# An MoE graph layer on one core: totals per expert ahead of the last ranks, and another order of the step loads

## The reference

```python
logits = tokens @ router_w.T
rw, re = jax.lax.top_k(softmax(logits), 2)
rw = rw / rw.sum(-1)
combine = zeros((N, E)).at[arange(N)[:, None], re].set(rw)
out = tokens
for e in range(8):
    h = gelu(tokens @ w1[e] + b1[e])
    y = h @ w2[e] + b2[e]
    out = out + combine[:, e:e + 1] * y
```

## Time and profile before

| | |
|---|---|
| median of 3 runs | 976.51 us (970.49 to 977.74) |
| the profiled execution, its own time | 976.27 us |
| its span, first to last instruction | 974.5 us |
| mean granted clock of TensorE | 0.933 of 2.4 GHz |
| TensorE (matmul) busy | 857.0 us, 88% |
| VectorE busy | 626.2 us, 64% |
| GpSimd busy | 723.4 us, 74% |
| ScalarE busy | 423.6 us, 43% |

### The profile page before, as it was taken

How to read it: one execution, slowest core, us unless ns; L and a number is a source line. 1 busy time by engine, 2 the same in 40 slices (tenths; PEclk the granted TensorE clock), 3 DMA queues, 4 the chain that set the end, 5 groups by cost and what they waited for, 6 DMA issues and landing times.

```text
span 974.5 us, 19961 instructions
## 1 busy us (share of the span) xinstructions
PE 857.0 (88%) x6332; PEld 528.3 (54%) x6332; DVE 626.2 (64%) x2219; ACT 423.6 (43%) x1156; POOL 723.4 (74%) x506
## 2 busy tenths in 40 slices
PE   3778887988999999999999999999939996499994
PEld 2433433444544454554554555555528996489993
DVE  3699998899466546446446465565666887555552
ACT  3544644333354433434433334344314554167763
POOL 4787888888887887887787888878851156567785
PEclk7699998897899999999999999999969998599997
DMA  9766475445564465454555547563395464568884
GB/s 301 163 111 110 53 144 85 63 60 88 95 126 78 66 116 93 73 84 73 94 84 90 96 57 135 76 124 35 40 301 171 136 192 145 165 111 133 134 136 58
DMA packets 150946, 109.50 MB, mean 112 GB/s; under 512 B 107415, under 2 KB 139354, under 8 KB 150716
## 3 DMA queue, kind: packets, MB, share of 16 engines
q0 software_dynamic: 62496, 26.49, 30.0%
q1 hardware_dynamic: 82272, 71.54, 25.9%
q10 hardware_dynamic: 6076, 10.20, 3.0%
HBM read 65.60 MB, written 42.73 MB: 111 GB/s over the span
## 4 chain that ended last, share of the span: by engine, by line
PE 33%; POOL 13%; issue 5%; DVE 4%; DMA 4%; SPq 1%; ACT 0%; POOLq 0%; DVEq 0%; ACTq 0%
POOL edge_sums L740 13%; PE ps L1585 5%; PE ps L1596 5%; PE ps L1374 4%; PE ps L1514 3%; DMA edge_sums<-sums,addr 3%; PE ps L1181 2%; PE ps L1361 2%; PE ps L1310 2%; PE ps L1324 2%; PE ps L1504 2%; PE ps L1570 1%; PE ps L1350 1%; DMA sums<-edge_sums 1%; PE ps L1249 1%
## 5 line engine op out<-in xcount | busy, mean ns | idle before, releaser
L740 POOL DMA_INDIRECT edge_sums<-sums,addr x360 | 566.2, 1573 | 136.9 <-issue 107.1
L1737 DVE TENSOR_SCALAR oh<-node,dsrc 128x500 bf16<-128x500 int16 (+1 forms) x392 | 116.4, 358 | 73.5 <-PE ps L1374 73.2
L981 ACT ACTIVATE r<-ps 128x500 f32<-128x500 f32 (+1 forms) x224 | 103.4, 549 | 72.0 <-PE ps L1310 71.9
L1374 PE MATMUL ps<-oh,r2t 128*64 128x500 bf16 (+1 forms) x1176 | 130.7, 359 | 1.4 <-DVE oh L1737 1.4
L1181 PE MATMUL ps<-edges,same 128*128 128x65 f32 x720 | 101.4, 287 | 12.5 <-ACT sums L814 4.6
L785 POOL DMA_INDIRECT out_x<-r x56 | 87.8, 1568 | 33.1 <-DVE r L2123 21.4
L1181 PEld LDWEIGHTS ps<-edges,same 128*128 128x128 f32 x720 | 92.1, 200 | 35.8 <-issue 28.1
L1700 DVE TENSOR_TENSOR r2t<-ps,r 125x4096 f32<-125x4096 f32 x25 | 110.3, 4412 | 0.0
L1640 DVE SCALAR_TENSOR_TENSOR same<-srow,src_f,below 128x128 f32<-128x128 int32 x360 | 103.6, 344 | 2.6 <-DMA srow<-in_src_row 1.4
L1374 PEld LDWEIGHTS ps<-oh,r2t 128*64 128x64 bf16 x1176 | 59.1, 110 | 71.2 <-issue 39.2
L1228 PE MATMUL ps<-r2t,r 125*32 125x512 f32 x400 | 60.3, 729 | 34.2 <-DVE r2t L1700 34.2
(11 more groups left out here) (296 smaller groups left out, 1356.3 us busy)
## 6 DMA issues: line engine op xcount, KB each, us to landing
srow<-in_src_row SPq DMA_DIRECT2D x45, 512.0 KB
edges<-in_edge_attr SPq DMA_DIRECT2D x22, 512.0 KB
r<-routed_rows SPq DMA_DIRECT2D x56, 129.0 KB
r<-hpre_rows SPq DMA_DIRECT2D x12, 500.0 KB, 4.5
edge_sums<-sums,addr POOLq DMA_INDIRECT x360, 3.3
r2t<-in_ew SPq DMA_DIRECT2D x4, 1024.0 KB, 8.9
hpre_rows<-r ACTq DMA_DIRECT2D x16, 250.0 KB, 2.3
edge_sums<-r SPq DMA_DIRECT2D x4, 884.0 KB, 13.8
```

Of the source, the lines that this page charges most:

```text
L740: pool.indirect_dma_start(out=tables[k], out_offset=bass.IndirectOffsetOnAxis(ap=addr[:, j:j + 1], axis=0), in_=sums[:, j % OR, :], in_off ...
L981: act.activation(phT[:, R % 2, h, 0:n], bank(BP[h], 128, 0, n), ACT.Square).then_inc(pair_squares, 1)
L1374: m = mm(ps[EA * a:EA * (a + 1), BD * BANK:BD * BANK + n], lhsT=parts3[:, (DCH - 1 - 2 * w // DW) * DW + (2 * w + a) % DW, s, :], rhs=oh[: ...
L1737: v.tensor_scalar(oh[:, (2 * i + a) % OHS, 0:nt * P].rearrange("p (t n) -> p t n", t=nt), node16[:, 0:nt, :], dsrc[:, 2 * w + a:2 * w + a ...
```

## The change

Seven edits go together.

- `carries` gets one more slot, the total behind the last batch. VectorE fills it with one add right behind the last `follow`, and the totals matmul on TensorE reads the three cuts and this slot instead of `carry` and the three cuts. It now stands ahead of the last `ranks`.
- The last `place` moves behind the whole table group, and no longer updates `carry`. TensorE waits for it (`meta_ready`) before the expert steps.
- SyncE no longer writes four pads ahead of the steps. It writes those of experts 0 and 2 behind the load of step 3; ScalarE writes the other six.
- SyncE reads a need at the steps 0, 4 and 6 only, and there takes the need of a later step (3, 5 and 6), which is not smaller. Step 7 waits for all rows (`rows_in` 4), where step 8 did.
- `turns` moves from step 1 to just behind `biases`, ahead of the steps.
- SyncE waits for the last table before it loads the hidden rows of the first four tiles, instead of between these and the weights.
- The two kept cuts move by one slot.

```diff
--- before.py
+++ after.py
@@ -53,6 +53,7 @@
     BASE = 16
     IDLE = E - 1
     EARLY = 8
+    NEEDS = {0: 3, 4: 5, 6: 6}
     SPARE = (0, 22, 44, 66, 88, 110, 128)
     CUTS = (1, 2, 3)
     LEAD = 8
@@ -251,7 +252,7 @@
         picked = carve([P, 2, most, E])
         rows_f = carve([P, 2, most])
         keeps = {n_: carve([P, E * n_]) for n_ in sorted({t1 - t0 for t0, t1 in BATCHES})}
-        carries = carve([P, 1 + len(CUTS), E])
+        carries = carve([P, 2 + len(CUTS), E])
         carry = carries[:, 0, :]
         runner = carve([P, T])
         red = carve([P, T])
@@ -610,10 +611,10 @@
             sp.wait_ge(x1_ready, NP * NB)
             for h in range(2):
                 sp.wait_ge(hpre_stored[h], 16 * MC * NB // 2)
+            sp.wait_ge(tables_back[G4 - 1], 32)
             load_hpre(0)
             load_hpre(1)
 
-            sp.wait_ge(tables_back[G4 - 1], 32)
             for k in range(KC):
                 for dst, w in ((ew1_s, ew1), (ew2_s, ew2)):
                     sp.dma_start(dst[:, k, :].rearrange("p (e n) -> p e n", e=E),
@@ -639,23 +640,28 @@
                     keep_rows(g)
 
 
-            sp.wait_ge(table_ready, 1)
-            for e in range(0, E, 2):
+            def put_pad(e):
+
                 row = sp.value_load(pad_row[0:1, e:e + 1], min_val=128 * IDLE, max_val=128 * IDLE + E * REG - 128)
                 sp.dma_start(routed[bass.ds(row, 128), :], pad_rows[:, :]).then_inc(pads_put, 16)
             sp.wait_ge(table_ready, 2)
 
             def load_steps(sts):
                 for s, h, nth in filter(some, sts):
-                    need = sp.value_load(need_i[0:1, s:s + 1], min_val=1, max_val=1 + 3) if s < EARLY else None
+                    if s in NEEDS:
+                        last = NEEDS[s]
+                        need = sp.value_load(need_i[0:1, last:last + 1], min_val=1, max_val=1 + 3)
                     row = sp.value_load(row_i[0:1, bass.ds(s, 1)], min_val=0, max_val=128 * IDLE + E * REG - 128)
-                    if s < EARLY:
+                    if s in NEEDS:
                         sp.wait_ge(rows_in, need)
-                    elif s == EARLY:
+                    if s == EARLY - 1:
                         sp.wait_ge(rows_in, 1 + 3)
                     wait(sp, xs_ps, s - (SB - 1))
                     wait(sp, idx_ready, s - (SB - 1))
                     sp.dma_start(xs[:, h, :], routed[bass.ds(row, 128), :]).then_inc(xs_loaded[h], 16)
+                    if s == 3:
+                        put_pad(0)
+                        put_pad(2)
                     allow(s - LEAD)
 
             def allow(s):
@@ -1111,7 +1117,7 @@
             act.preload_act_table(ACT.Gelu)
 
             act.wait_ge(table_ready, 1)
-            for e in range(1, E, 2):
+            for e in (1, 3, 4, 5, 6, 7):
                 row = act.value_load(pad_row[0:1, e:e + 1], min_val=128 * IDLE, max_val=128 * IDLE + E * REG - 128)
                 act.dma_start(routed[bass.ds(row, 128), :], pad_rows[:, :]).then_inc(pads_put, 16)
 
@@ -1552,12 +1558,13 @@
             tiles(gnn, 4, [(t1 + 6, lambda b=b: ranks(b)) for b, (t0, t1) in enumerate(BATCHES[:-1])])
             pe.wait_ge(hsum_ready, T)
             pe.wait_ge(x2_ready, T)
+            pe.wait_ge(carried, len(BATCHES))
+            mm(bank(7, 128, 0, (1 + len(CUTS)) * E), lhsT=ones[0:P, :], rhs=carries[:, 1:, :].rearrange("p a e -> p (a e)"), start=True, stop=True).then_inc(ranks_ps, 1)
             ranks(len(BATCHES) - 1)
-            pe.wait_ge(carried, len(BATCHES))
-            mm(bank(7, 128, 0, (1 + len(CUTS)) * E), lhsT=ones[0:P, :], rhs=carries.rearrange("p a e -> p (a e)"), start=True, stop=True).then_inc(ranks_ps, 1)
 
 
             pe.wait_ge(table_ready, 3)
+            pe.wait_ge(meta_ready, len(BATCHES))
             pe.wait_ge(ew_loaded, 16 * (2 * KC + 1))
 
             def xs_T(st):
@@ -2013,11 +2020,14 @@
                 t0, t1 = BATCHES[b]
                 n_ = t1 - t0
                 pk = picked[:, :, 0:n_, :]
-                v.wait_ge(ranks_ps, b + 1)
+                final = b == len(BATCHES) - 1
+                v.wait_ge(ranks_ps, b + 1 + final)
                 link(v.tensor_tensor(pk, bank(0, P, 0, n_ * E).rearrange("p (t e) -> p t e", e=E).unsqueeze(1)
                                      .to_broadcast([P, 2, n_, E]), chosen[:, :, t0:t1, :], ALU.mult))
                 link(v.tensor_reduce(rows_f[:, :, 0:n_], pk, AX.X, ALU.add))
                 v.tensor_copy(row_idx[0:P, :, t0:t1], rows_f[:, :, 0:n_]).then_inc(meta_ready, 1)
+                if final:
+                    return
                 v.wait_ge(meta_ready, b + 1)
                 v.tensor_tensor(carry, carry, upto[:, 0:E * n_].rearrange("p (e t) -> p e t", e=E)[:, :, n_ - 1], ALU.add).then_inc(carried, 1)
                 v.wait_ge(carried, b + 1)
@@ -2045,18 +2055,22 @@
             last_b = len(BATCHES) - 1
             lead(last_b)
             follow(last_b)
+            v.wait_ge(mask_ready, len(BATCHES))
+            n_last = BATCHES[-1][1] - BATCHES[-1][0]
+            v.tensor_tensor(carries[:, 1 + len(CUTS), :], carry, upto[:, 0:E * n_last].rearrange("p (e t) -> p e t", e=E)[:, :, n_last - 1],
+                            ALU.add).then_inc(carried, 1)
             weights(last_b)
-            place(last_b)
-
-            v.wait_ge(ranks_ps, len(BATCHES) + 1)
-            v.tensor_copy(pad_row[:, :], bank(7, 1, 0, E)).then_inc(table_ready, 1)
-            link(v.tensor_tensor(e_n, bank(7, 128, 0, E), reg_start[:, :], ALU.subtract))
+
+            v.wait_ge(ranks_ps, len(BATCHES))
+            total = bank(7, 128, len(CUTS) * E, (1 + len(CUTS)) * E)
+            v.tensor_copy(pad_row[:, :], total[0:1, :]).then_inc(table_ready, 1)
+            link(v.tensor_tensor(e_n, total, reg_start[:, :], ALU.subtract))
             link(v.tensor_scalar(e_i, e_n, 127.0, None, ALU.add))
             link(v.tensor_scalar(e_i, e_i, -128, None, ALU.bitwise_and))
             link(v.tensor_copy(e_pad, e_i))
             link(v.tensor_tensor_scan(e_end, ones[:, 0:E], e_pad, 0.0, ALU.mult, ALU.add))
             v.memset(first_row[:, 0:1], 0.0)
-            v.tensor_scalar(first_row[:, 1:3], bank(7, 1, 2 * E, 4 * E).rearrange("a (k e) -> a k e", k=2)[:, :, 0],
+            v.tensor_scalar(first_row[:, 1:3], bank(7, 1, E, 3 * E).rearrange("a (k e) -> a k e", k=2)[:, :, 0],
                             float(128 * IDLE + 127), None, ALU.subtract)
             v.tensor_scalar(e_n, e_pad, -1.0, float(REG), ALU.mult, ALU.add)
             link(v.tensor_scalar(step_row[:, :], step_row[:, :], e_end[:, E - 1:E], float(128 * NS), ALU.add, ALU.subtract))
@@ -2073,7 +2087,9 @@
             link(v.tensor_reduce(exp_f, past, AX.X, ALU.add))
             v.tensor_scalar(exp_i[:, :], exp_f[0:1, :], float(C), None, ALU.mult).then_inc(table_ready, 1)
             for at_, more in ((0, 256.0), (1, 128.0)):
-                v.scalar_tensor_tensor(cut_n[:, at_, :], bank(7, 1, (1 + at_) * E, (2 + at_) * E), more, reg_start[0:1, :], ALU.add, ALU.subtract)
+                v.scalar_tensor_tensor(cut_n[:, at_, :], bank(7, 1, at_ * E, (1 + at_) * E), more, reg_start[0:1, :], ALU.add, ALU.subtract)
+
+            place(last_b)
 
             def biases():
 
@@ -2137,13 +2153,12 @@
                     w1_copy(step_at(st, 2), cols[-1])
                     output_rows(st)
                     add_b2(step_at(st, -1), cols[-4])
-                    if st[0] == 1:
-                        turns()
             v.wait_ge(table_ready, 3)
             v.wait_ge(ew_loaded, 16 * (2 * KC + 1))
             for s in range(2):
                 w1_copy((s, s, 0), expert_of((s, s, 0)))
             biases()
+            turns()
             steps(v, expert_steps, SB, 2)
```

## The result

The changed kernel took 966.15 us (median of 6 runs, 960.39 to 967.86) where the kernel before took 975.74 in the same comparison (6 runs, 970.49 to 980.13): ratio 0.9894, 95% interval 0.9864 to 0.9924. That is 9.6 us, more than twice the forecast 3.9, and just under the low end of the range (967.5). The profiled execution's own time is 966.35, its span 964.6.

A forecast was written before the change was run, and what follows sets the result against it. TensorE limits most of the span, with a hole between routing and expert steps filled by SyncE's queue. Terms of -3.8 and 0 on 976.27 gave 972.5, with the median's 0.24 972.7; forecast 972.6, range 967.5 to 977.1.

The forecast's parts named there:

- Part 1: Totals ahead of the last ranks: all tables behind the last count scan come 2.26 us earlier.
- Part 2: SyncE's new order: step 0's load issued 3.07 us earlier, at 834.55; first transposes at 837.3 instead of 840.39.
- The cover for place: Last batch's row indices come later, but GpSimd reaches that batch only at 838.46, leaving 4 us of cover.
- needs, pads and step 4: Coarser needs and the moved pads cost nothing, as long as step 4's load keeps 2 us of slack.
- Part 3: Waits table ahead of the steps: copy 2 at 844.8, hidden layer 2 2.5 us earlier (bounds 1.0 and 2.9).
- the 2.31 ahead of layer 4: TensorE's 2.31 us wait at 855.40 for VectorE, made by the waits table in step 1; forecast to go.
- Part 4: Hidden-row reload behind the last table's landing: forecast 0, with -1.5 and +1.5 us as bounds.
- The clock's term: Rise to the higher level at about 850.2: layer 4 gains 4.8 if it moves along, 3.6 if not; taken -3.8.
- rival (1): Clock rises before the wait for copy 2; layer 2 and output 0 run faster, another 1.2: -6.0 us; chance 0.22.

The follow-up runs named there:

- a_reuse_2: Changed kernel in which VectorE keeps the expert registers of the first two weight copies instead of rereading them: 968.41 us, ratio 0.9945 to the kernel before.
- b_warm: Kernel before plus 24 matmuls of 128x128 that nobody reads, behind the totals matmul in TensorE's idle stretch: 974.33 us, ratio 1.0011.

## Why the prediction was wrong

**The steps, one by one.** Part 1 forecast 2.26 us for the tables: 3.27 - 0.99 = 2.28. Part 2 forecast 3.07 for step 0: issued at 830.92, 7.2 behind the scan, instead of 10.4, 3.2 earlier; the transposes 2.96. The cover for place held (5 us; 4 forecast), and needs, pads and step 4 cost nothing. Part 3 forecast copy 2 at 844.8, 17.6 behind the old scan, and 1.6 us of waiting: 17.0 and 1.07, with three loads at 0.59 instead of 0.7. Hidden layer 2 came 2.9 earlier (2.5 forecast, bound 2.9), and the 2.31 ahead of layer 4 went. Part 4 forecast 0, and no effect is shown. The Trainium skill, "DMA: Bandwidth & Descriptors", section "Queues, rings and completion order", says that each DMA engine consumes a queue's descriptors in ring order; by it the order of reload and table makes no odds to the table. The means to the table's add, 16.0 against 15.2 us with a standard error of 0.5, neither bear that out nor contradict it.

**The step that failed: the clock, taken as one value.** The sum took one rise from one profile (850.2) and asked only whether it moves with the work: 3.6 or 4.8, hence 3.8. The clock's term in it is a loss: layer 4 moves by 2.5 + 2.31 = 4.8 without it and by 3.8 with it, so +1.0. In the compared pair the clock rose 16.3 behind the scan instead of 23.0, and hidden layer 4 moved 6.45 = 2.94 + 2.31 + 1.2: the term was a gain of 1.2, as rival (1) had it. But that pair set a late rise against a lucky one. The rise of the old step order alone lay between 18.0 and 23.0, that of the new between 14.3 and 21.5, and the ends lay 2.8 and 1.6 us apart. Also missing was the other direction: the clock can fall again behind a standstill. Averaged over four profiles of either order the region gives 3.8, give or take 0.8. That it equals the forecast is luck: the term is a spread of some 1 to 1.5 us to either side of an execution, and not a number. The Trainium skill, "TensorE: Matmul & The Clock Gate", "Part 1: The HAM clock gate", says that the number of matmuls before the rise varies from run to run of one kernel. The three profiles of the changed kernel agree in that the time of the rise varies with the same instructions (14.3, 14.5 and 16.3 behind the scan).

The other 3.5 of the pair's 9.9 us between spans lie ahead of the scan. The sum put that stretch at nothing apart from the reload, as if every execution came to the scan at the same time. Three profiles of the changed kernel alone have the scan's end at 823.7, 826.4 and 830.3.

**The range built on it was too narrow.** Its low end allowed for "a run that is 1.5 us under its median" and stood on a median of three runs, 976.51. Over all comparisons, 109 runs of the kernel before average 974.0 and 30 of the changed kernel 968.05, with standard errors of 0.3 and 0.6: the change is worth 5.9 us, give or take 1.3. Without the first comparison, which raised the question, 103 and 24 runs give 5.1, give or take 1.3. The first comparison had six runs on either side, one group 1.8 above its average and the other 2.9 below. Between their means lie 10.5 us, 4.6 too much, from groups whose standard errors are 1.3 and 1.2: far out, but the two repeats had the same code and did not show it. To that extent the miss was bad luck. Had the sum been put on 974.0, the forecast would have been 970.2.

**What stays open.** 5.9 in the timed runs stand against 3.8 in the profiles of the step region and 4.5 with the scatters cut. The difference of 2.1 is about twice its joint error, and that of the repeats alone, 1.3, about as large as its own. Whether the reload or the choice of executions to profile makes it is not settled: in the 15 profiles with all edge scatters the scan ends at 826.8 on average with the old order of the reload and at 824.9 with the new one, but 1.25 of these 1.8 us stand at the last edge scatter already, ahead of any changed line, and the standard error is 1.5. Why the clock differs between executions of the same instructions isn't shown either.

## What to carry to other kernels

Before a sum of 4 us is made, look at how far two profiles of the same kernel lie apart in the stretch that is changed, and place it from a common event (here the last count scan), not from the start of the span. A wait inside a row of steps costs its own length and, in some executions (here four of seven), the work behind it at the lower clock level; removing it was worth about 3 us in two profiles where 2.3 were on the page. Two gains that both end at the same wait (copy 2) don't add in full.

## What the runs showed of the hardware

The time of an execution goes with TensorE's mean granted clock, though the code is the same: over 103 runs of the kernel before the correlation is -0.69, over 30 of the changed one -0.85, with 0.4 and 0.7 us less for each 0.001 of clock. Which of the two drives the other is not shown. One place where it differs lies far ahead of the change. Windows of before, then of a_reuse_2, over code that both share:

```profile
225.00:250.00 25.00, 20.83 (x202) 13.94 (x202) 18.02 (x58) 9.96 (x23) 21.04 (x14) 0.66 0.51 80
```

```profile
225.00:250.00 25.00, 19.60 (x184) 12.46 (x186) 15.91 (x52) 8.16 (x18) 21.04 (x14) 0.86 0.61 103
```

The clock was 0.66 in 14 of 18 profiles and 0.86 in two, a_reuse_2 and b_warm; these two had their last edge scatter at 698.7 and 700.7, every other kernel with all scatters between 702.8 and 708.3.

24 matmuls on an idle TensorE brought the rise forward to 8.8 us behind the scan, but the clock fell at 15.5 and rose again at 19.0, and the time stayed as it was (ratio 1.0011). And three register loads in a row took 1.78 us of VectorE, 0.59 each; each took longer than the weight copy behind them (0.48).
